# A three-stage decoder layer: norm scales in pairs, a residual sum behind a norm, and another PSUM bank for one product

## What is computed

```python
# stage 1 (attn): two-column potential -> Green function -> x1; decayed linear attention -> x; gelu FFN
x = _layernorm(x + _L0_attn_ref(x, ...))          # holds xn1, xn2, xn3 = layernorm(...) inside
# stage 2 (xattn): cross attention of 16 heads of 8 columns against ctx_1024, with a key mask
x = _layernorm(x + _L0_xattn_ref(x, ctx_1024, ctx_1024, mask, ...))
# stage 3 (ffn): router logits = x @ Wr.T, the top 2 of 8 experts by softmax, each expert a gelu FFN
x = _layernorm(x + _L0_ffn_ref(x, ...))
```

## Time and profile before

| | us |
|---|---|
| median of 3 runs | 768.02 (767.54 to 770.93) |
| profiled execution, its time | 772.6 |
| its span, first to last instruction | 770.7 |
| one group of the loop, chosen to chosen | 60.2 to 60.4 |
| last group, chosen to chosen | 64.2 |
| TensorE's granted clock in the loop | full (2.4 GHz) |
| from 537.2 to 595.2 us | half (1.2 GHz) |

### The profile page before, as it was taken

One profiled execution on the slowest core, in us unless ns is written; L12 is line 12 of the kernel. 1 busy time (PEld: TensorE's weight loads), 2 busy tenths in 40 slices (PEclk: granted clock), 3 DMA queues, 4 the chain that ended last, 5 costly groups with the idle time before them and its releaser, 6 DMA issues.

```text
span 770.7 us, 19904 instructions
## 1 busy us (share of the span) xinstructions
PE 658.1 (85%) x6190; PEld 495.3 (64%) x6190; DVE 505.1 (66%) x1733; ACT 400.8 (52%) x855; POOL 321.6 (42%) x463
## 2 busy tenths in 40 slices
PE   9879898899998998998999989985867999999920
PEld 8664756755755754764764764763643999999920
DVE  4587568768678669668668678774525555545535
ACT  0212365474475375475475565553420777767716
POOL 6104362363354264264165156145014355544535
PEclk7579999999999999999999999996558999999975
DMA  8600000000000000000000000000023322222144
GB/s 286 220 1 14 2 30 16 2 25 14 4 25 14 4 23 13 7 21 14 7 21 11 11 12 20 11 0 29 2 110 90 78 74 73 72 64 68 54 166 180
DMA packets 26058, 36.23 MB, mean 47 GB/s; under 512 B 7302, under 2 KB 18311, under 8 KB 25736
## 3 DMA queue, kind: packets, MB, share of 16 engines
q1 hardware_dynamic: 20582, 22.72, 9.6%
q0 software_dynamic: 4576, 9.53, 3.6%
q10 hardware_dynamic: 850, 3.38, 1.3%
HBM read 23.99 MB, written 12.63 MB: 48 GB/s over the span
## 4 chain that ended last, share of the span: by engine, by line
PE 51%; DVE 15%; issue 12%; POOL 9%; ACT 6%; DMA 2%; SPq 1%; DVEq 1%; ACTq 1%; POOLq 0%
PE bank L1561 9%; PE bank L1876 8%; PE bank L1886 7%; PE bank L1726 4%; POOL rstd L737 4%; ACT mix L555 3%; PE bank L1597 3%; PE bank L1713 3%; PE bank L1695 3%; PE bank L1645 2%; PE bank L1653 2%; PE bank L1484 2%; POOL vare L734 1%; PE bank L1734 1%; POOL expert_in L779 1%
## 5 line engine op out<-in xcount | busy, mean ns | idle before, releaser
L779 POOL DMA_INDIRECT expert_in<-xb_rows,slot_u x72 | 73.3, 1018 | 102.5 <-PE bank L1704 48.9
L871 POOL DMA_INDIRECT expert_out<-xa,v_sb x71 | 68.5, 965 | 79.3 <-issue 43.0
L675 ACT ACTIVATE hT<-bank,qT 128x128 f32<-128x128 f32 x284 | 81.2, 369 | 38.0 <-PE bank L1876 20.3
L734 POOL TENSOR_SCALAR vare<-mv 128x1 f32<-128x1 f32 (+1 forms) x108 | 23.9, 221 | 168.2 <-DVE mv L1064 167.8
L1186 DVE TENSOR_REDUCE negmax<-bank 128x4 f32<-128x512 f32 x128 | 79.4, 683 | 8.6 <-PE bank L1695 8.6
L555 ACT ACTIVATE mix<-bank 128x512 f32<-128x512 f32 x128 | 66.1, 604 | 23.4 <-PE bank L1713 23.4
L1886 PE MATMUL bank<-w_t,hT 128*128 x568 | 75.8, 276 | 1.6 <-ACT hT L675 0.6
L1876 PE MATMUL bank<-xnT,qT 128*128 128x128 f32 x568 | 75.2, 275 | 1.1 <-DVE qT L1400 1.1
L1886 PEld LDWEIGHTS bank<-w_t,hT 128*128 128x128 f32 x568 | 69.1, 192 | 2.8 <-issue 2.5
L737 POOL TENSOR_TENSOR rstd<-vare,minus_half 128x1 f32<-128x1 f32 (+1 forms) x108 | 66.5, 615 | 9.6 <-POOL vare L734 1.2
L1876 PEld LDWEIGHTS bank<-xnT,qT 128*128 128x128 f32 x568 | 69.0, 192 | 1.6 <-DVE qT L1400 1.6
(11 more groups left out here) (300 smaller groups left out, 1461.4 us busy)
## 6 DMA issues: line engine op xcount, KB each, us to landing
v_sb<-expert_in SPq DMA_DIRECT2D x71, 66.0 KB
w_t<-in_w_t ACTq DMA_DIRECT2D x1, 2064.0 KB, 7.4
x_all<-in_x SPq DMA_DIRECT2D x4, 512.0 KB, 7.9
xT_all<-in_xT SPq DMA_DIRECT2D x4, 512.0 KB, 8.6
ctxT<-in_ctxT SPq DMA_DIRECT2D x8, 256.0 KB
w_t<-in_w_t SPq DMA_DIRECT2D x1, 2048.0 KB, 7.4
x_all<-expert_out SPq DMA_DIRECT2D x4, 512.0 KB, 10.0
mix<-expert_out SPq DMA_DIRECT2D x3, 512.0 KB, 7.2
```

The lines of the kernel that those rows point to most:

```text
L675: ins = nc.scalar.activation(hx[j % 2][:, c, :], bank[2 + j % 2][:, c * P:(c + 1) * P], ACT.Gelu, bias=w1c[j % 2][:, FF + c:FF + c + 1])
L779: nc.gpsimd.indirect_dma_start(xs[:, :], bass.IndirectOffsetOnAxis(ap=slot_u[:, t, k:k + 1], axis=0), xb_rows[k][:, t, :], None).then_inc( ...
L871: nc.gpsimd.indirect_dma_start(ys[:, :], bass.IndirectOffsetOnAxis(ap=tag[j % ROWS][:, HOME - P:HOME - P + 1].bitcast(U32), axis=0), ysb[j ...
```

## The change

Five edits. The LNA scales are made in two calls of two tiles instead of four of one; so are the LNB scales. POOL gets a further wait, for the four LN3 norms of group g + 1, ahead of group_sum. On DVE the last LN3 norm moves ahead of the index search. The product xo2 moves from bank 6 to bank 2, so that PER_GROUP becomes 11, 14, 12, 11, 16, 14, 13, 12.

```diff
-                            "17254206176306451035274"))))
+                            "17254206172306451035274"))))
...
-                ln_scale(LNA, g, 0)
-                ln_scale(LNA, g, 1)
-                ln_scale(LNA, g, 2)
-                ln_scale(LNA, g, 3)
+                ln_scale(LNA, g, 0, 2)
+                ln_scale(LNA, g, 2, 2)
...
-                for t in range(T):
-                    ln_scale(LNB, g, t)
+                ln_scale(LNB, g, 0, 2)
+                ln_scale(LNB, g, 2, 2)
                 if not last:
                     ln_scale(LN3, g + 1, 1)
                     ln_scale(LN3, g + 1, 2)
                     ln_scale(LN3, g + 1, 3)
+                    pool.wait_ge(xn_ready[LN3], ln_nth(g + 1, T - 1) + 1)
                     group_sum(g + 1)
...
+                if not last:
+                    heb_norm(g + 1, 3)
                 for t in range(T):
                     ins = nc.vector.max_index(top_i[:, t, :], top8[:, t, :], lg[:, t, :])
                 ins.then_inc(route_link, 1)
-                if not last:
-                    heb_norm(g + 1, 3)
```

## The result

The changed kernel is slower: 775.75 us median of 6 runs (774.01 to 777.83) against 767.78 (767.45 to 770.93), a ratio of 1.0098, 95% interval 1.0071 to 1.0126. The forecast was 768.7 in a range that ended at 773.0. Its profiled execution has a span of 774.4 us.

What follows compares the result with a forecast made beforehand. PE was taken as the bound, released by chosen at the FFN. Per-group losses of 0.09 + 0.09, LNA gains and first and last group terms summed to +0.7 on 768.02, giving 768.7 us, range 763 to 773.

Steps and rivals of the forecast that it cites:

- The sum: Whole kernel: chosen and PE row +1.3, LNA -0.7, first group +0.4, last group +0.35 - 0.65; together +0.7 us.
- So the FFN starts 0.77 behind chosen, whatever the norm ahead does: FFN start: PE must finish the rank product and loop branch after chosen, so an earlier LN3 norm doesn't help.
- The cast: Router on DVE: top_f's cast is held until group_sum ends, making chosen 0.09 us later per group.
- LNB scales: Ahead of the xb_rows transposes: pairs bring the fourth norm 0.5 us earlier, 0.41 after one register row.
- the bank and the scales uncover each other: At xo2 and the xb_rows norms: without the bank wait the norms set PE's time, so both were priced together, 0.41 earlier.
- rival (d): LNA and LNB scales: a two-column power costs 1.05 us like a four-column one; time near 776, chance 0.07.
- LNA scales: FFN start to fourth xa norm: PE goes on after 12.62 instead of 12.74, 0.12 us gained in six groups.
- The bank and the register rows: xo2's bank and threshold rows on PE and DVE: bank gains nothing alone; one exposed PE row loses 0.09 a group.
- The bank alone would bring nothing: At xo2: without the bank 6 wait PE would wait for the xb_rows norm instead, no gain.
- Rival (c): PE's register rows: all twelve exposed at 0.09 us, 7 us in all, 775.6 us; chance 0.11.

Runs made afterwards that it cites:

- e1: Kernel before with only xo2 moved from bank 6 to bank 2; 769.23 us, ratio 1.0043.
- e3: Kernel before with only the LNA and LNB scales made in pairs; 764.58 us, ratio 0.9978.
- e4: Kernel before with only the last LN3 norm ahead of the index search and group_sum waiting for that norm; 773.18 us, ratio 1.0093.
- e6: e4 plus a filler, six matmuls that nothing reads, ahead of PE's wait for chosen; 768.21 us, ratio 0.9987.
- e2: Changed kernel with xo2 back on bank 6; 774.67 us in four runs, ratio 1.0105.
- e7: Kernel before with only the last LN3 norm ahead of the index search, group_sum not waiting for it; 774.23 us, ratio 1.0067.
- e9: Kernel before with only the last context turn (ctT3) moved from bank 2 to bank 6; ratio 1.0012.
- e17: Kernel before with only the last context turn (ctT3) moved from bank 2 to bank 6, third run of this kernel; ratio 1.0009.
- e13: Changed kernel unaltered, rerun on a chip of the second kind; 767.29 us, ratio 1.0086.
- e15: Changed kernel with the last context turn (ctT3) on bank 6, restoring the banks' job counts of before; 769.50 us, ratio 1.0101.
- e16: Changed kernel plus the filler of six unread matmuls ahead of PE's wait for chosen; 756.94 us, ratio 0.9963.
- e12: Changed kernel with the last context turn on bank 6 (counts of before) and group_sum behind POOL's wait for chosen; 754.71 us, ratio 0.9932.
- e8: Kernel before with both scales in pairs, xo2 on bank 2 and the last context turn on bank 6; 764.92 us, ratio 0.9965.
- e5: Kernel before with xo2 on bank 2 and, in exchange, the last context turn on bank 6, keeping the job counts; 767.84 us, ratio 0.9982.
- e14: Kernel before with only the last context turn (ctT3) moved from bank 2 to bank 6, second run of this kernel; ratio 1.0010.
- e18: Same kernel as e12, on another run: counts of before, group_sum behind POOL's wait for chosen; 755.69 us, ratio 0.9942.
- e10: Changed kernel plus the filler of six unread matmuls ahead of PE's wait for chosen; 757.60 us, ratio 0.9979.
- e11: Changed kernel plus the filler, with the last context turn on bank 6 (counts of before); 759.18 us, ratio 0.9985.

## Why the prediction was wrong, step by step

From the first mask to the seventh, six groups (windows; "late" is from the end of the first context product to its drain; the chip of before and the change is counted with the first kind by its times and drains):

| kernel | chips | us | half-clock stretches | late |
|---|---|---|---|---|
| before | first kind | 361.69 | 0 | 0.4 |
| e1, bank | first | 364.60 | 0 | 1.1 |
| e3, pairs | first | 358.77 | 0 | 0.4 |
| e4, order | first | 368.18 | 4 | 0.4 |
| e6, order, filler | first | 360.86 | 0 | 0.4 |
| e2, order, pairs | first | 366.60 | 3 | 0.4 |
| e7, order, sum not waiting | first | 367.87 | 3 | 0.4 |
| the change | first | 369.47 | 3 | 1.1 |
| e9, last turn on bank 6 | second | 359.74 | 1 | 0.07 |
| e17, the same kernel | second | 358.38 | 0 | 0.07 |
| the change (e13) | second | 365.33 | 5 | 0.07 |
| the change, counts of before (e15) | second | 367.49 | 6 | 0.07 |
| the change, filler (e16) | second | 356.47 | 0 | 0.07 |
| e12 | second | 352.96 | 0 | 0.07 |

**The sum, the step that failed.** The forecast was +0.7 us and the change cost 8.0, in the loop 4.9 by half-clock stretches and 2.9 by the late drain. The sum priced every edit in time on the path and put the effect on TensorE's clock at nothing, without a reason. "So the FFN starts 0.77 behind chosen, whatever the norm ahead does" is right for its start (0.75 measured) and wrong for its speed: with the norm ahead, PE's two short waits became one of 1.64 us, and 3.4 us at the start of the FFN ran at half clock in three to six groups of a run, 1.5 to 1.7 us each. Shown by e4 and e6, and by e13 and e16 in the changed kernel itself. What decides which groups are struck stays open. The granted clock stood in the columns of the earlier trace rows; I read only that it was full in the loop.

**The cast.** Right: held, 0.90 us, the norm 0.34. The forecast had the mask 0.09 late although the pairs start its chain 0.41 early; e4 has no pairs, and its mask comes 0.47 later against the logits, which fits 0.09 + 0.41. What I gave no number in the order edit is its other side: the next group's POOL chain starts earlier, so that e4's groups without a stretch are no longer than before's.

**LNB scales.** The size is right: 0.5 was forecast and 0.41 left behind a register row of the bank edit; e3, without that edit, shows 0.49. That the bank and the scales uncover each other is not: the pairs gain as much with PE's wait for bank 6 in place (e3) as without it (e8). The power of two columns takes 0.71 to 0.73 us where 0.74 was taken, so rival (d) is out.

**LNA scales.** Wrong in sign where it counts. In e3 the fourth xa norm comes 12.99 behind the mask for 12.92, nothing gained for the 0.12 forecast. The forecast compared its 12.62 with one row, 287.62, at which PE had waited 0.43; in the groups beside it the wait is 0.30 and the transpose comes 0.13 earlier against the mask, which is the whole of the gain. And behind the order edit singles reach 12.47 (e4) where pairs stay at 12.97 (e2). DVE and POOL of e4, then of the changed kernel:

```profile
349.06 0.56 POOL L737 TENSOR_TENSOR rstd<-vare,minus_half 128x1 f32<-128x1 f32 x1
...
349.66 0.41 DVE L1069 TENSOR_SCALAR xa<-x,mv,rstd 128x128 f32<-128x128 f32 x1 [0.50 <-POOL rstd L737]
```

```profile
349.85 0.33 POOL L734 TENSOR_SCALAR vare<-mv 128x2 f32<-128x2 f32 x1 [1.01 <-DVE mv L1063]
350.33 0.71 POOL L737 TENSOR_TENSOR rstd<-vare,minus_half 128x2 f32<-128x2 f32 x1 [0.15 <-POOL vare L734]
...
351.08 0.66 DVE L1067 TENSOR_SCALAR xa<-x,mv,rstd 128x128 f32<-128x128 f32 x2 [0.94 <-POOL rstd L737]
```

POOL stands idle for 1.01 us until both tiles of the pair are there. By these rows the LNA pair gives back the 0.5 that the LNB pair earns: e2's groups without a stretch take 60.2, like e4's. That the change would be better with single LNA scales is argued from these rows; no kernel tried it.

**The bank and the register rows.** "The bank alone would bring nothing" is 0.49 us a group too kind on the first kind of chip (e1), where the sum had one register row of 0.09; on the second kind the bank edit never ran alone. Rival (c) had the right size (0.49 a group is five or six rows at 0.09) and the wrong shape: it is no "issue" time, whose share fell from 12% to 9%, but completions that come late, the first context's by 0.7 us and the second's by 0.3, for which PE waits. Their cause is not settled. That they came with the changed numbers of jobs, and went when these were restored (e1 against e5), speaks for the counts and the register rows that they place; but these two ran on two chips, and the run that would decide (e9, e14, e17) never met a chip of the first kind. Nor is it shown that the chip makes the difference and not the hour: no chip showed both behaviours, but the first two served only the first eight runs, the others only the later ones.

**Of the range:** with the half-clock stretches left out, the change costs 2.9 us from mask to mask on the first kind of chip, which would be near 770.7, inside 763 to 773. It is what the bank edit costs alone (e1). On the second kind the changed kernel with the filler gains a little (e16, 0.9963). The half-clock stretches are worth 5 to 10 us by themselves.

## What to carry to other kernels

An edit that makes a short task early may move idle time rather than remove it: add up what the busiest engine's waits become, and if two short ones join ahead of dense matmuls, look at the granted clock behind them, since a wait can cost more in the work that follows than in itself. Handing a pair over together is good where its consumer is late anyway and, by the rows above, bad where the engine has to wait for the second input. A gain that is read from one group should be compared with the groups beside it. Before crediting a delay to a dependency, compare it on a second chip.

## What the runs showed of the hardware

- TensorE was granted half clock, 1.2 GHz, for 3.4 us behind 1.64 us of idle in otherwise dense work, in three to six of six groups. It was so too behind 0.64 and 0.99 in three (e7), behind 0.64 and 0.31 in one of six (e9, e14) or none (before and five others), and never behind 0.90 (e12, e18) or 0.26 with a filler (e6, e10, e11, e16). Which groups are struck differs from run to run.
- Chips seem to differ. On the first kind the drain of a group's first context product (32 matmuls) begins 0.4 us behind its modelled end, or 1.1 with the bank edit, and the fourth's always 0.06; on the second kind all begin 0.07 behind. One kernel was traced on both, the changed one: 1.1 and 0.07. Before takes 767 to 769 us on the first and 760 on the second.
- A VectorE norm with one SBUF tile as input that was issued just behind the start of a GpSimd sum took 1.29 us, one that met it later 0.74, one outside it 0.34, and a cast of 128x8 0.90 for 0.17: the three that were held ended within 0.1 us of the sum's end.
